# The FFNs' probabilities turned by transposing transfers, not by TensorE, with scores, product with v and context sum at other experts

## The reference

```python
x = x + 0.5 * ffn(layernorm(x))
x = x + attention(layernorm(x))      # 16 heads, 4 groups, causal
x = x + 0.5 * ffn(layernorm(x))

def ffn(y):                          # E = 16 experts, C = 256, H = 128
    w = gate(y)                      # (tokens, 16), a softmax over chosen experts
    q, k, v = (sum_e w[:, e] * (y @ proj[e]) for proj in (q_proj, k_proj, v_proj))
    s = causal(q @ k.T / sqrt(H))    # within each of the 8 batch items
    ao = softmax(s) @ v
    return sum_e (w[:, e] * ao) @ o_proj[e]
```

## Time and profile before

| what | value |
|---|---|
| median of 3 runs | 2606.5 us (2606.39 to 2609.38) |
| the profiled execution | 2606.3 us, its span 2604.5 us |
| PE (matmul) busy | 2512.5 us, 96% of the span |
| DVE busy | 2151.8 us, 83% |
| ACT busy | 945.6 us, 36% |
| POOL busy | 909.6 us, 35% |
| mean granted clock of TensorE | 0.989 of full speed |

### The profile page before, as it was taken

One profiled execution on the slowest core, in us unless ns is written; L12 is line 12 of the kernel. 1 busy time (PEld: TensorE's weight loads), 2 busy tenths in 40 slices (PEclk: granted clock), 3 DMA queues, 4 the chain that ended last, 5 costly groups with the idle time before them and its releaser, 6 DMA issues. The chain is left out here.

```text
span 2604.5 us, 45222 instructions
## 1 busy us (share of the span) xinstructions
PE 2512.5 (96%) x14116; PEld 2298.7 (88%) x14116; DVE 2151.8 (83%) x6164; ACT 945.6 (36%) x2546; POOL 909.6 (35%) x1950
## 2 busy tenths in 40 slices
PE   6999999999997999999999999997999999999998
PEld 6999999999995888888888888886899999999997
DVE  6888888888886888888888888886888888888887
ACT  3111111101103777777777777774101101101100
POOL 4332332332323434343434344334332322323321
PEclk9999999999998999999999999998999999999999
DMA  6000000000001554554545554555000000000000
GB/s 191 13 1 1 1 1 1 1 1 1 1 25 50 91 91 92 92 92 92 89 90 88 90 92 92 89 96 136 25 9 1 9 9 1 9 9 1 9 9 9
DMA packets 378736, 117.25 MB, mean 45 GB/s; under 512 B 338561, under 2 KB 377473, under 8 KB 378497
## 3 DMA queue, kind: packets, MB, share of 16 engines
q1 hardware_dynamic: 378496, 114.36, 22.0%
HBM read 26.24 MB, written 4.19 MB: 12 GB/s over the span
## 5 line engine op out<-in xcount | busy, mean ns | idle before, releaser
L555 PE MATMUL ffn_ring<-ffn_mix_weights,ffn_yT 128*128 128x384 f32 x5760 | 1157.2, 342 | 5.9 <-DVE ffn_mix_weights L790 3.4
L555 PEld LDWEIGHTS ffn_ring<-ffn_mix_weights,ffn_yT 128*128 128x128 f32 x5760 | 1009.1, 190 | 56.7 <-DVE ffn_mix_sums L725 15.8
L727 DVE SCALAR_TENSOR_TENSOR ffn_mix_sums<-ffn_ring,ffn_w,ffn_mix_sums 128x384 f32<-128x384 f32 x896 | 550.6, 615 | 244.1 <-PE ffn_ring L555 227.5
L605 PE MATMUL ffn_ring<-ffn_out_weights,ffn_avT 128*128 128x512 f32 x1536 | 442.9, 399 | 6.3 <-POOL ffn_avT L1028 4.5
L1547 ACT ACTIVATE attn_exponentials<-attn_exponentials,attn_score_neg_max 128x512 f32<-128x512 f32 (+3 forms) x512 | 285.7, 559 | 164.3 <-DVE attn_score_neg_max L1462 163.7
L1615 POOL CAST attn_probsT_long<-attn_turned_long 128x1024 fp32r<-128x1024 f16 (+1 forms) x256 | 232.5, 936 | 251.1 <-DVE attn_probs L1479 250.4
L605 PEld LDWEIGHTS ffn_ring<-ffn_out_weights,ffn_avT 128*128 128x128 f32 x1536 | 283.0, 189 | 36.2 <-POOL ffn_avT L1028 5.7
L1479 DVE SCALAR_TENSOR_TENSOR attn_probs<-attn_exponentials,attn_prob_factor,attn_probs 128x512 f16<-128x512 f32 (+3 forms) x512 | 248.2, 546 | 15.5 <-ACT attn_probs L1556 15.2
L1556 ACT ACTIVATE attn_probs<-attn_exponentials,attn_prob_factor 128x512 f16<-128x512 f32 (+3 forms) x512 | 250.0, 552 | 23.1 <-DVE attn_prob_factor L1472 15.6
L742 DVE SCALAR_TENSOR_TENSOR x<-ffn_ring,ffn_w_out,x 128x256 f32<-128x256 f32 x512 | 247.1, 483 | 13.0 <-PE ffn_ring L605 6.5
L1302 PE MATMUL attn_scores<-attn_kT,attn_qT 128*128 128x512 f32 (+2 forms) x1152 | 242.8, 338 | 4.7 <-DVE attn_qT L1445 3.2
(11 more groups left out here) (149 smaller groups left out, 3262.4 us busy)
## 6 DMA issues: line engine op xcount, KB each, us to landing
ffn_mix_stage<-in_L_ffn_q_proj_dram SPq DMA_DIRECT2D x32, 128.0 KB, 2.5
ffn_mix_stage<-in_L_ffn_k_proj_dram SPq DMA_DIRECT2D x32, 128.0 KB, 2.5
ffn_mix_stage<-in_L_ffn_v_proj_dram SPq DMA_DIRECT2D x32, 128.0 KB, 2.8
ffn_out_stage<-in_L_ffn_o_proj_dram SPq DMA_DIRECT2D x16, 256.0 KB, 2.9
out_dram<-x SPq DMA_DIRECT2D x8, 512.0 KB, 2.9
x<-in_L_attn_x_dram SPq DMA_DIRECT2D x7, 512.0 KB, 8.3
early_stage<-in_L_attn_w_q_dram SPq DMA_DIRECT2D x4, 512.0 KB, 5.2
attn_dense_stage<-in_L_attn_w_dense_dram SPq DMA_DIRECT2D x4, 512.0 KB, 4.8
```

The source lines that it names most:

```text
L555: last = pe.matmul(bank[:, 0:QKV], yT[:, t % 2, h, k * P:(k + 1) * P], mix_half(e, wh)[:, k], start=(n == 0), stop=(n == 3 * CK - 1))
L605: last = pe.matmul(bank[:], avT[:, t % 2, h], wo[:, g, wh], start=(i == 0), stop=(i == 2))
L727: dve.scalar_tensor_tensor(into, bank[:, 0:QKV], w[:, t, e:e + 1], into, ALU.mult, ALU.add).then_inc(mix_done, 1)
```

## The change

For tiles 1 to 30 of each FFN (`by_dma`) the probabilities are no longer turned by TensorE. ACT writes a float16 high part of the probabilities, scaled by 2^15 (`prob16_high`), DVE the float16 low part (`prob16_low`), SP starts one transposing transfer for both parts (`turn_probs`), and POOL casts what landed to float32r (`cast_turned`). The weights of the output take the factor 2^-15. Tiles 0 and 31 stay as they were. For tiles 1 to 30 the scores move from e = 6 to e = 5, `attend` from 12 to 13, and `sum_av` from 13 to 14. The buffers `prob` and `probT` are shared with the new float16 buffers.

```diff
+def by_dma(T):
+
+    return 0 < T < TILES - 1
+
...
+            def turn_probs(T):
+
+                columns = 2 * (T % QT + 1) * P
+                sp.wait_ge(pt_lo, T + 1)
+                sp.dma_start_transpose(turned[:, 0:columns].rearrange("p (j q) -> p j q", q=P),
+                                       prob16[:].rearrange("p j h k -> p (j h k)")[:, 0:columns]).then_inc(t_landed, 16)
...
             def attend(T, t):
 
-                pe.wait_ge(pt_hi, T + 1)
-                pe.wait_ge(pt_lo, T + 1)
+                if by_dma(T):
+                    pe.wait_ge(pt_free, T + 1)
+                    pe.wait_ge(av_done, T)
+                else:
+                    pe.wait_ge(pt_hi, T + 1)
+                    pe.wait_ge(pt_lo, T + 1)
                 pe.wait_ge(v_lo, T + 1)
...
-                    if e == 6 and inside(T, 1):
+                    if inside(T, 1) and e == (5 if by_dma(T - 1) else 6):
                         scores(T - 1, (t + 3) % QT)
-                    if e == 9 and inside(T, 1):
+                    if e == 9 and inside(T, 1) and not by_dma(T - 1):
                         transpose_probs(T - 1, (t + 3) % QT)
-                    if e == 12 and inside(T, 1):
+                    if inside(T, 1) and e == (13 if by_dma(T - 1) else 12):
                         attend(T - 1, (t + 3) % QT)
...
+            def prob16_low(T, t):
+                n = (t + 1) * P
+                dve.wait_ge(pt_hi, T + 1)
+                dve.scalar_tensor_tensor(prob16[:, 0:t + 1, 1], prob[:, 0:n].rearrange("p (j k) -> p j k", k=P), PROB_SCALE,
+                                         prob16[:, 0:t + 1, 0], ALU.mult, ALU.subtract).then_inc(pt_lo, 1)
+
...
-                        if e == 7:
+                        if e == (6 if by_dma(T - 1) else 7):
                             score_max(T - 1, prev)
+                        if e == 8 and by_dma(T - 1):
+                            prob16_low(T - 1, prev)
                         if e == 9:
                             prob_rsum(T - 1, prev)
-                        if e == 10:
+                        if e == 10 and not by_dma(T - 1):
                             split_probs(T - 1, prev)
                         if e == 11:
                             output_weights(T - 1, prev)
-                        if e == 13:
+                        if e == (14 if by_dma(T - 1) else 13):
                             sum_av(T - 1, prev)
...
+            def prob16_high(T, t):
+                n = (t + 1) * P
+                act.wait_ge(exp_done, T + 1)
+
+                act.wait_ge(av_ready, T)
+                act.activation(prob16[:, 0:t + 1, 0], prob[:, 0:n].rearrange("p (j k) -> p j k", k=P), ACT.Copy,
+                               scale=PROB_SCALE).then_inc(pt_hi, 1)
...
+            def cast_turned(T, t):
+                pool.wait_ge(t_landed, 16 * T)
+
+                pool.wait_ge(av_ready, T)
+                pool.tensor_copy(pT[:, 0:t + 1].rearrange("p j h q -> p (j h q)"),
+                                 turned[:, 0:2 * (t + 1) * P]).then_inc(pt_free, 1)
...
                 if inside(T, 1):
+                    if by_dma(T - 1):
+                        cast_turned(T - 1, prev)
                     split_av(T - 1, prev)
```

More of the change, by code:

```diff
@@ L48 @@
 ON_POOL = (5, 7, 13)
+PROB_SCALE = 2.0 ** 15
 class Resident:
@@ L304, in ffn @@
         stage_out = sb("out_stage", [P, STAGE_OUT, 2 * C])
+        turned = nc.alloc_sbuf_tensor_at(f"{name}_prob_turned", [P, 2 * SEQ], F16, offset=nc.sbuf_base)
+        prob = sb("prob", [P, SEQ])
+        prob16 = nc.alloc_sbuf_tensor_at(f"{name}_prob_halves", [P, QT, 2, P], F16, offset=nc.sbuf_base)
+        pT = sb("probT", [P, QT, 2, P], F32R)
         stats = sb("ln_stats", [P, 2, 6])
@@ L476, in _ @@
                 load_out(g)
-            if aw:
-                for n in range(EARLY):
-                    if n == 0:
-                        split_done(sp, E + OG - 2)
-                        split_done(sp, E + OG - 1)
-                    if n == 2:
-                        last_tile_past(sp, aw.first_end)
-                    if n == EARLY - 2:
-                        last_tile_past(sp, aw.second_end)
-                    src, _, _, _, width = aw.pieces[n]
-                    raw = aw.parts(n)[0]
-                    sp.dma_start(raw, src).then_inc(aw.loaded[n % EARLY], 16)
+            def turn_probs(T):
[3 more added lines that the diff above has]
+                                       prob16[:].rearrange("p j h k -> p (j h k)")[:, 0:columns]).then_inc(t_landed, 16)
@@ L489, in _, with load_early @@
+            def load_early(n):
+                if n == 0:
+                    split_done(sp, E + OG - 2)
+                    split_done(sp, E + OG - 1)
+                if n == 2:
+                    last_tile_past(sp, aw.first_end)
+                if n == EARLY - 2:
+                    last_tile_past(sp, aw.second_end)
+                src, _, _, _, width = aw.pieces[n]
+                sp.dma_start(aw.parts(n)[0], src).then_inc(aw.loaded[n % EARLY], 16)
             if out is not None:
@@ L490, in _, with store @@
                 out_rows = out.rearrange("b (t p) c -> b p t c", p=P)
[L491 to L494 removed]
+            def store(b):
+                sp.wait_ge(x_merged, b * QT + QT)
+                sp.dma_start(out_rows[b], m.x[:, b * QT:b * QT + QT, :]).then_inc(stored, 16)
@@ L495, in _ @@
+            for T in range(1, TILES - 1):
+                if aw and T == TILES - 2:
+                    for n in range(EARLY - 2):
+                        load_early(n)
+                turn_probs(T)
+                if out is not None and T > QT and T % QT == 1:
+                    store((T - QT) // QT)
+            if aw:
+                load_early(EARLY - 2)
+                load_early(EARLY - 1)
+            if out is not None:
+                store(B - 1)
                 sp.wait_ge(stored, 16 * B)
@@ L756, in score_max @@
                 dve.wait_ge(scores_ready, T + 1)
-                reach(dve, pt_tr, T)
+                reach(dve, pt_free, T)
                 settle(dve)
@@ L930, in slot @@
                         gate_exp(T + 1, (t + 1) % QT)
-                    if e == 7 and inside(T, 1):
+                    if inside(T, 1) and e == (6 if by_dma(T - 1) else 7):
                         exponentials(T - 1, (t + 3) % QT)
-                    if e == 9 and inside(T, 1):
+                    if e == 7 and inside(T, 1) and by_dma(T - 1):
+                        prob16_high(T - 1, (t + 3) % QT)
+                    if e == 9 and inside(T, 1) and not by_dma(T - 1):
                         split_probs(T - 1, (t + 3) % QT)
@@ L1088 @@
 LAST_LAG = 4
-PROB_SCALE = 2.0 ** 15
 PROB_AT = (0, P, 3 * P, 6 * P)
```

15 lines of the change are left out of this document (5 added, 10 removed).

## The result

The changed kernel's median is 2591.2 us over 6 runs (2588.75 to 2595.07), that of the kernel before, run beside it, 2606.3 us over 6 (2603.33 to 2609.38). The ratio is 0.9943, with a 95% interval of 0.9933 to 0.9953: 15.1 us less. The forecast was 2592.8, in a range of 2588 to 2602.

What follows compares the result with a forecast made beforehand. PE, busy for 500.00 of 500.00 us, was taken to set the FFNs' time. Removed blocks 18.0, less 4.1 at the border and 0.2 in slot 32, gave 13.7 us off the median 2606.5: 2592.8, range 2588 to 2602.

Steps and rivals of the forecast that it cites:

- Turned blocks removed: On PE in both FFNs: 150 blocks at 0.10 us and 60 sets at 0.05 disappear, 18.0 us less.
- The scores and the product with v at other experts: On PE: the same matmuls at other places in the slot, priced at nothing.
- The road: Probabilities from DVE's low part through transfer and POOL's cast to PE: hidden with 1.2 us to spare, landing 3.1.
- The border: Between slots: later context sum makes DVE's sum of expert 0 0.07 us late, 58 times; 4.1 us, bounds 0 and 8.7.
- The cover of this wait is used up: Expert 2's mixture load waiting for DVE: 0.22 us more waiting gave 0.18 more time, so counted one for one.
- Slot 32: No mixture lies between; first projections wait some 0.7 us, but PE waits for q and k anyway: 0.2 us for both FFNs.
- Late probabilities: Rival, chance 0.12: at `attend` of wide tiles, 5.4 us landings come too late; 19 us slower, 2626.
- The fuller border: Rival, chance 0.10: between slots, reciprocal waited out and context's parts 0.1 us late; 12 us come back, 2600.
- No price at the border: Rival, chance 0.05: sum of expert 0 comes as before, or DVE runs ahead; 18 us less, 2588.5.

Runs made afterwards that it cites:

- Moves alone: Kernel before, TensorE's turned blocks kept, scores, maximum and exponential one expert sooner, product with v and context sum one later: 2605.8 us, ratio 1.0001.
- taking the sum ahead: Changed kernel with the context's two DVE instructions before the sum of expert 14 again, product with v unmoved: 2589.7 us, ratio 0.9937 to the kernel before.
- naming the bank's last reader: Changed kernel with expert 2's mixture waiting for pair 7's output sums instead of the sum of expert 0: 2584.0 us, ratio 0.9914 to the kernel before.
- The repeat: The changed kernel run again unaltered, beside its variants: 2589.1 us, ratio 0.9939 to the kernel before.
- the product sooner: Changed kernel with the product with v at expert 12 and the context sum at 13, as before the change: 2594.1 us, ratio 0.9952 to the kernel before.

## Why the prediction was right

**Turned blocks removed: 18.0 us forecast, 17.5 measured.** By the trace of before, the steps with 1, 2, 3 and 4 blocks take 2.93, 3.00, 3.13 and 3.23 us, those without 2.78: 0.15, 0.22, 0.35 and 0.45 more; the line through the first and the last gave 0.15, 0.25, 0.35 and 0.45. With their counts 14, 16, 16 and 14 the sum is 17.5. The kernel with blocks turned twice put 16.1 (slots) to 18.4 (medians) on the same blocks.

**The scores and the product with v at other experts: nothing forecast, nothing measured.** Moves alone, which include the border, gave a ratio of 1.0001 and 0.8 us in the 56 slots, and that is no more than the border's price.

**The road: hidden, 1.2 us to spare forecast, 1.4 measured.** From the issue of 8 blocks to the start of the cast 3.15 us pass, POOL's wake-up among them, where the forecast had 3.2; SP's wake-up took 0.03 instead of 0.1, and the low part 0.68 instead of 0.76. The forecast's words count a projection too many in what PE does meanwhile; its sum of 7.3 has the right three. The figure of the Trainium skill ("VectorE: DVE Perf Modes", "The three transpose paths", 1309 ns for one 128x128 turn by DMA) doesn't add up block after block here: the trace disagrees with 8 times that, since 8 blocks are there within 3.15 us of the issue. (By that figure 6 blocks would be 3.2 us beyond the room, 7.85 less 4.67, and not 3.3.) The Trainium skill's rule ("VectorE: DVE Perf Modes", "Rules for kernel authors") to turn on TensorE where PSUM may receive it would give the 15 us back here, since PE, busy for 96% of the span, is what this kernel lacks.

**The border: 4.1 us forecast, some 2 measured.** This is the term that was mis-sized. The forecast moved every instruction of DVE's row by the durations of the earlier trace rows and came to 0.07 us; here a few of the starts came 0.01 us sooner than that, which leaves 0.03 at the sum of expert 0, 0.04 at the load, and 0.03 to 0.04 in the slot's length. A difference of 0.07 made from seven rows that are rounded to 0.01 can't be better than that. The mechanism and its place were right: taking the sum ahead gives back 0.03 to 0.04, and naming the bank's last reader takes the whole wait away. "The cover of this wait is used up" holds too: of a wait of 0.27 us 0.17 is covered and 0.10 counts. One thing stays open: slots of four blocks show their whole 0.45, as if the border cost nothing there, while the others fall 0.04 to 0.06 short of what their blocks cost.

**Slot 32: 0.2 forecast for both FFNs, some 0.05 measured.** The timeline of PE there, before and then changed, second FFN, from the projection of pair 7 to the turn of q and k:

```profile
2574.97 2.27 PE L605 MATMUL ffn_ring<-ffn_out_weights,ffn_avT 128*128 128x512 f32 x9
2578.29 0.44 PE L565 MATMUL ffn_transposes<-ident,ffn_qkv 128*128 128x128 f32 x2 [1.05 <-POOL ffn_qkv L1012]
```
```profile
2564.15 0.86 PE L637 MATMUL ffn_ring<-ffn_out_weights,ffn_avT 128*128 128x512 f32 x3
2565.61 1.67 PE L637 MATMUL ffn_ring<-ffn_out_weights,ffn_avT 128*128 128x512 f32 x6 [0.59 <-POOL ffn_avT L1085]
2567.50 0.44 PE L593 MATMUL ffn_transposes<-ident,ffn_qkv 128*128 128x128 f32 x2 [0.22 <-POOL ffn_qkv L1062]
```

The first projection waits 0.59 for the context's parts, and the wait for q and k behind it falls from 1.05 to 0.22: 3.32 us from one start to the other before, 3.35 now, and 3.32 and 3.34 in the first FFN. That is the forecast's mechanism, 0.6 where it said 0.7; a new wait of 0.59 costs next to nothing where an old one gives way.

**The sum.** 15.2 us by the slots, 15.1 by the medians, 13.7 forecast. With the terms as measured it is 17.5 - 2.2 = 15.3. The forecasts by slot were 0.38, 0.28, 0.18 and 0.08; 0.45, 0.30, 0.16 and 0.11 came.

**The rivals.** Late probabilities came about only with a second landing on the road. The fuller border's second part, the context's parts late, came about only one expert later. No price at the border (2588.5) was the nearest of them: the median after is 2591.2, and half of the border's price did not come. The repeat's 2589.1 is even nearer to that rival than to 2592.8, so the time alone does not decide between the two; the load's longer wait and the slots given back by the sum ahead do.

## What to carry to other kernels

Where PE is full, price a removed set of matmuls by the starts of its neighbours with and without it, and look for the next wait in the queue of the engine that takes the moved step: here 0.03 to 0.04 us a slot at the border, 2 in all, was nearly all that came back of 17.5. A transfer that replaces PE's work is free only within the distance between its last producer and its first reader; write that distance down for each step of the road, since one expert (1.7 us) to either side cost 5 or 100 us. And a wait of 0.2 us in each of 60 slots is worth a look at what it really needs: naming the bank's last reader instead of the next instruction in the queue brought 5 us, a third of what the whole change did.

## What the runs showed of the hardware

**The clock at an FFN's start scatters, and with it the run.** The second FFN's slot 0 took 27.67 us before and 29.46 in the changed kernel, with the same instructions in it. Windows over it, before and then changed (clock third from the end):

```profile
1796.64:1824.31 27.67, 23.12 (x99) 19.88 (x99) 23.83 (x42) 13.86 (x23) 17.51 (x29) 0.84 0.61 177
```
```profile
1791.65:1821.11 29.46, 24.38 (x99) 20.97 (x99) 24.09 (x42) 13.85 (x23) 17.34 (x29) 0.76 0.59 170
```

The granted clock is a mix of the two levels (1.2 and 2.4 GHz) in both, 0.84 and 0.76. Over the eleven profiled executions (before, changed and the nine others) this slot took 27.7 to 28.8 us in the six with a clock of 0.80 to 0.85, and 28.3 to 29.8 in the five with 0.76 to 0.78. Kernels with the change lie in both groups (three and five), the three without it all in the first; whether that is chance is not shown. The next slot, slot 1 of the second FFN, is the clearest: 21.0 us in the five executions with a clock of 1.00, 22.3 to 22.5 in the six with 0.92. In the first FFN slot 1 took 23.2 us in one execution of the changed kernel and 21.3 in the other, at 0.93 and 1.00. The attention, whose code is the same in all, took 927 to 932 us from the first to the last of its projections of z; its clock reads 1.00 before and after alike, and the cause of that scatter stays open. The two executions of the changed kernel, 6.0 us apart, differ by 2.7 in slots 0 and 1 of the first FFN and by 3.3 between the last turn of y in the first FFN and the first in the second. In slots 0 and 1 of both FFNs and in that stretch the changed kernel's profiled execution lost 4.0 us against before, and so the profiled pair shows 11 us where the medians show 15.

**A transfer's landing is a start and a small price per block.** 2, 4, 6 and 8 blocks of 128x128 float16 land in 2.3, 2.4, 2.7 and 3.0 us at the least, 8 of them were cast from 3.15 us after the issue in the slot shown, and two transfers of 8 in series took 6.47.

**Single landings are longer, and some of them at the same place each time.** In slot 24 of the first FFN (8 blocks) the landing took 3.9 us in the changed kernel, in its repeat, with the bank's wait edited, with the product sooner and with the doubled transfer; in slot 12 of the second FFN 3.5 to 3.7. With every step one expert later the same two slots had 3.1 and 3.0. What they meet there is not known. In the changed kernel the room covered them all.
